# Local-attention layers: VectorE's chain of inverse norms issued behind the maximum and subtraction of the scores

## The reference

```python
def attn_layer(x, Wqkv, qs, ksc, Wo):
    q, k, v = jnp.split(x @ Wqkv, 3, -1)          # 16 heads of 64 each
    q = l2norm(q) * qs                            # t / max(norm(t), 1e-12), per head
    k = l2norm(k) * ksc
    q = q * cos * scale + rotate_half(q) * sin * scale
    k = k * cos * inv + rotate_half(k) * sin * inv
    out = local_attention(q, k, v)                # window 32, keys of this and the last window
    return out.transpose(0, 2, 1, 3).reshape(b, n, INNER) @ Wo

for i in range(DEPTH):                            # 6 layers
    x = attn_layer(shift_tokens(x), Wqkv[i], q_scale[i], k_scale[i], Wo[i]) + x
    x = ffn_layer(shift_tokens(x), ln_g[i], ln_b[i], W1[i], b1[i], W2[i], b2[i]) + x
```

## Time and profile before

| what | value |
|---|---|
| median of 3 runs | 4396.46 us (4378.6 to 4422.52) |
| the profiled execution | 4409.03 us |
| its span, first to last instruction | 4407.3 us |
| part B in it | about 1024 to 4330 us |
| mean granted TensorE clock | 0.906 of full speed |
| TensorE busy with matmuls | 3998.6 us, 91% |
| VectorE busy | 3520.4 us, 80% |
| GpSimd busy | 2552.0 us, 58% |
| ScalarE busy | 2544.9 us, 58% |

### The profile page before, as it was taken

How to read it: one execution, slowest core, us unless ns; L and a number is a source line. 1 busy time by engine, 2 the same in 40 slices (tenths; PEclk the granted TensorE clock), 3 DMA queues, 4 the chain that set the end, 5 groups by cost and what they waited for, 6 DMA issues and landing times. The chain is left out here.

```text
span 4407.3 us, 153325 instructions
## 1 busy us (share of the span) xinstructions
PE 3998.6 (91%) x66018; PEld 2914.3 (66%) x66018; DVE 3520.4 (80%) x5436; ACT 2544.9 (58%) x4654; POOL 2552.0 (58%) x1429
## 2 busy tenths in 40 slices
PE   7899999986998999999999999999999999999996
PEld 4555555545776777777776777777776777777774
DVE  5655555536888889999988898999988889998993
ACT  4544555534555666656656566666665566666563
POOL 2333333326666676667666666667766666666662
PEclk7866666658999999999999999999999999999997
DMA  1000000001211122221211122122121111212112
GB/s 46 4 3 2 2 2 2 3 26 41 54 49 48 48 54 55 53 56 48 62 54 47 49 54 54 52 56 56 48 54 52 51 54 49 56 50 53 50 48 61
DMA packets 122834, 188.19 MB, mean 43 GB/s; under 512 B 24910, under 2 KB 44134, under 8 KB 121964
## 3 DMA queue, kind: packets, MB, share of 16 engines
q1 hardware_dynamic: 122220, 179.07, 15.0%
HBM read 23.78 MB, written 4.19 MB: 6 GB/s over the span
## 5 line engine op out<-in xcount | busy, mean ns | idle before, releaser
L1251 POOL TENSOR_TENSOR rc<-rc,rnorm 128x1024 f32<-128x1024 f32 x384 | 734.5, 1933 | 358.5 <-DVE rnorm L205 358.5
L1245 POOL TENSOR_TENSOR rc<-rc,rs 128x1024 f32<-128x1024 f32 x384 | 905.2, 2369 | 34.5 <-DVE rs L1313 30.8
L1273 POOL TENSOR_TENSOR prob_b<-prob_b,rinv 128x1024 f32<-128x1024 f32 x192 | 365.9, 1906 | 653.0 <-DVE rinv L1386 653.0
L562 POOL TENSOR_TENSOR prob<-prob,rden 128x512 f32<-128x512 f32 (+3 forms) x128 | 297.6, 2325 | 661.3 <-DVE rden L674 661.3
L1307 DVE TENSOR_TENSOR rc<-proj,rope_b 128x1024 f32<-128x1024 f32 x384 | 469.2, 1222 | 114.9 <-PE proj L853 63.8
L941 PE MATMUL ring<-pT,vmoved 64*64 64x32 f32 x18432 | 436.0, 221 | 115.1 <-issue 113.8
L1093 ACT ACTIVATE oT_b<-ring 128x512 f32<-128x512 f32 x384 | 209.6, 596 | 564.6 <-PE ring L941 564.6
L941 PEld LDWEIGHTS ring<-pT,vmoved 64*64 64x64 f32 x18432 | 401.0, 135 | 179.5 <-issue 162.3
L890 PEld LDWEIGHTS ring<-ident,rc 128*128 128x128 f32 x3072 | 362.3, 143 | 235.5 <-POOL rc L1251 77.2
L890 PE MATMUL ring<-ident,rc 128*128 128x128 f32 x3072 | 455.9, 278 | 62.2 <-POOL rc L1251 59.4
L1321 DVE TENSOR_REDUCE sums<-squares 128x16 f32<-128x1024 f32 x384 | 460.2, 1198 | 44.5 <-ACT squares L1105 42.3
(11 more groups left out here) (163 smaller groups left out, 8837.0 us busy)
## 6 DMA issues: line engine op xcount, KB each, us to landing
vmoved<-vown SPq DMA_DIRECT2D x576, 128.0 KB, 2.4
vmoved<-vown SPq DMA_DIRECT2D x192, 192.0 KB, 2.5
vmoved<-vown SPq DMA_DIRECT2D x576, 64.0 KB, 2.1
wqkv_raw<-in_L_ffn_Wqkv SPq DMA_DIRECT2D x40, 192.0 KB, 2.7
wo<-in_L_ffn_Wo SPq DMA_DIRECT2D x6, 512.0 KB, 4.2
x_attended<-xtok SPq DMA_DIRECT2D x8, 256.0 KB, 2.0
xtok_c<-x_attended SPq DMA_DIRECT2D x8, 256.0 KB, 4.4
out<-xtok_c SPq DMA_DIRECT2D x8, 256.0 KB, 2.5
```

The source lines that it names most:

```text
L1245: nc.gpsimd.tensor_tensor(rc[:, k % 2, c, :], rc[:, k % 2, c, :], rs[:, c, :], ALU.add).then_inc(add_done, 1)
L1251: nc.gpsimd.tensor_tensor(dst, dst, rnorm[:, k % 2, c * HEADS:(c + 1) * HEADS].rearrange("p (h o) -> p h o", o=1).broadcast_to([P, HEADS, ...
L1273: nc.gpsimd.tensor_tensor(pr, pr, rinv[:, :, :].rearrange("p q (s o) -> p q s o", o=1).broadcast_to([P, PAIRS, 2, KEYS]), ALU.mult).then_i ...
```

## The change

In VectorE's list of every step, the call of `norms_of(g + 1, ...)` is moved from in front of the maximum and subtraction of tile g to behind them. Nothing is added, removed or resized, and the lists of the other engines stay as they are.

```diff
                 if tile(g + 1):
                     square_sums(1, g + 1)
-                if tile(g + 1) or seq_at(g, 6) is not None:
-                    norms_of(g + 1, seq_at(g, 6))
                 if tile(g):
                     dve.wait_ge(scr_full, g + 1)
                     nc.vector.tensor_reduce(rmax[:, :, :], scr[:, :, :, :], AX.X, ALU.max).then_inc(max_done, 1)
@@
                         prob[g % 2][:, :, :, :].rearrange("p q s k -> p s q k"), scr[:, :, :, :],
                         rmax[:, :, :].rearrange("p s (q o) -> p s q o", o=1).broadcast_to([P, 2, PAIRS, KEYS]),
                         ALU.subtract).then_inc(sub_done, 1)
+                if tile(g + 1) or seq_at(g, 6) is not None:
+                    norms_of(g + 1, seq_at(g, 6))
```

## The result

The changed kernel takes 4629.03 us (median of 4 runs, 4593.07 to 4641.46), the kernel before beside it 4409.49 us (4 runs). The ratio is 1.0494, 95% interval 1.0403 to 1.0585: slower, as forecast (4646 us; 1.057 of the median then shown). In a second job it was 4614.6 us, ratio 1.063 (1.0531 to 1.0729). Medians are of all runs, but a ratio takes only those within 1.5% of the fastest run of their kernel, which in the second job, by one run of 4310.12 us, are 5 of the 17 of the kernel before: there the medians themselves (4614.6 and 4380.57 us) have a ratio of 1.053. The profiled execution has a span of 4615.0 us at a mean clock of 0.902.

A forecast was written before the change was run, and what follows sets the result against it. Bound: TensorE back to back, caught at times by the chain norms, `scale_heads`, T1. Chain 205 plus clock 45 is 250 us on the profiled 4409, 4659; less 12.6 for the median, 4646 us, range 4546 to 4760.

The forecast's parts named there:

- The clamp: VectorE's clamp in its new place takes 0.18 us instead of 1.84, bounds 0.18 and 1.84.
- The chain behind the scores: Tiles 1 and 3: next masks 8.91 us after the scores end; steps grow by 2.38 and 1.55 us.
- The reserve of one tenth for covered waits: Pauses in `weigh` cover some of the new wait, so nine tenths of 225 us: 205 us.
- Tile 2: `spread` (L978), in front of the output projection, waits for the later copy: +0.76 us per sequence.
- one of the prediction's own signs of being wrong: In any step, scores ending earlier in their step than in the kernel before would make the prediction wrong.
- the sentence that what is freed comes back nowhere: TensorE, ScalarE and VectorE's rotations regain nothing elsewhere from what the change frees; no time credited.
- The clock: Behind TensorE's 96 new waits at T0 and T1, three in ten cost 1.6 us each: 45 us, from 0 to 154.
- tile 0's: Tile 0's step: the chain ends at 2918.76, masks were at 2918.80 anyway, so 0 added.
- B: Rival: VectorE bounds tiles 2 and 0, so its saving of 1.66 us each shortens them; 4237 us, chance 0.04.
- C: Rival: the clamp's 1.84 us is its own and moves with it into the chain; 4938 us, chance 0.05.
- D: Rival: most of TensorE's 147.6 us of pauses in `weigh` vanish; 4453 us or less, chance 0.05.

The follow-up runs named there:

- the norms in the middle: Against the kernel before: order maximum, norms, subtraction in all tiles; 4454.19 us, ratio 1.0183.
- the wait alone: Against the kernel before: its order kept, only a wait for the scores put in front of the norms; 4410.07 us against 4402.94, ratio 1.005.
- filled, second run: Changed kernel plus unused products in front of T0 and T1 in TensorE's waits of tiles 1 and 3, run again; 4525.43 us, ratio 1.0447 to the kernel before.
- the first experiment: Against the kernel before: norms behind maximum and subtraction only in tiles 1 and 3; 4612.53 us, ratio 1.051.
- low part later: Against the kernel before: GpSimd's second low part of the input (L1227) moved behind the scaling of the next step; 4359.18 us against 4377.84, ratio 1.0003.
- both edits: Against the kernel before: clamp left out and GpSimd's second low part moved behind the next scaling; 4355.02 us against 4380.57, ratio 1.0019.

## Why the prediction was right

The direction, the mechanism and the total came out; the terms of the sum did not all have their size. The total is closer than the forecast was: 250 us more were forecast and 219.5 measured (4629.03 - 4409.49). 4646 lies 17 us from 4629 because the median it was added to, 4396.46 us, was 13 us below the one measured beside the changed kernel. That is luck.

**The clamp.** Taken at 0.18 us, measured 0.171. That its 1.84 us were a stall behind GpSimd's add was argued from the ends of both; the runs without the clamp and with the add moved show it. One reading was off: what ends at 2861.39 in tile 1 is not an add of the halves but GpSimd's L1287 (from 2860.12), beside which the first guess took its 1.20 us. The time given to the clamp doesn't change by it.

**The chain behind the scores.** 8.91 us were predicted from the end of the scores to the next masks. In the step of tile 1 above, the last scores start at 2966.16 and take 0.86 us, as the next fence shows, and the masks come at 2975.82: 8.80 us. Tile 1 was to grow by 2.38 us and grew by 2.26 in the median, tile 3 by 1.55 and grew by 1.45. The reserve of one tenth for covered waits was about right too: 114 and 74 us before it, 102.6 and 71.5 measured. The experiment with the norms in the middle shows the slope, the one with the wait alone that it is the work behind the scores and not the wait.

**Tile 2** is the term that was mis-sized: +0.76 us through `spread`. In the changed kernel TensorE (first and last row) and VectorE read:

```profile
2966.16 0.86 PE L910 MATMUL scr<-kT,qT 64*32 64x64 f32 x64
...
2982.65 0.86 PE L910 MATMUL scr<-kT,qT 64*32 64x64 f32 x64
...
2983.55 1.22 DVE L1399 TENSOR_REDUCE rmax<-scr 128x16 f32<-128x1024 f32 x1 [0.74 <-PE scr L910]
...
2988.04 0.43 DVE L1343 COPY hid<-rnorm 128x512 f32<-128x512 f32 x1
...
2988.53 0.66 PE L978 MATMUL proj<-ident,hid 128*128 128x128 f32 x4 [0.26 <-DVE hid L1343]
```

The wait is there, but 0.26 us long, and it came in 26 of the 48 tiles 2, 12.1 us in all. The scores end 7.69 us into the step (2983.51 - 2975.82), in the kernel before 8.12. That the scores end earlier in their step was one of the prediction's own signs of being wrong; it came true in tile 2. In the kernel before, TensorE's weight loads wait twice in this step for ScalarE to empty a bank:

```profile
2868.22 0.42 PEld L890 LDWEIGHTS ring<-ident,rc 128*128 128x128 f32 x4 [0.31 <-ACT qT L1093]
...
2871.09 0.19 PEld L851 LDWEIGHTS ring<-wqkv_hi,xa_hi 128*128 128x128 f32 x1 [0.56 <-ACT qT L1093]
```

In the same step of the changed kernel neither wait is there: while TensorE waits in tile 1, VectorE and ScalarE get ahead. So the sentence that what is freed comes back nowhere was wrong. The medians of the steps that no low clock touches separate the two effects (us):

| kernel | tile 1 | tile 2 | tile 3 | tile 0 |
|---|---|---|---|---|
| before | 16.00 | 17.41 | 16.98 | 16.79 |
| norms behind only in tiles 1 and 3 | 18.27 | 17.07 | 18.43 | 16.66 |
| norms behind only in tiles 0 and 2 | 15.71 | 17.97 | 16.96 | 16.97 |
| changed | 18.27 | 17.55 | 18.43 | 16.62 |
| filled, second run | 18.27 | 17.56 | 18.43 | 16.61 |

A longer tile 1 alone gives tile 2 back 0.34 us, the late copy alone costs it 0.56, and both together 0.14.

**The clock** was taken somewhat too small: 45 us. Between the two kernels that ran side by side, the time at the low clock fell by 190 us (259 to 69) and part B by 84. That makes 0.44 us per us at the low clock; between the first traces of the two it was 65 us of part B for 140 at the low clock, 0.46. The changed kernel has 118 us more at it than the kernel before (114 to 232), in the second job 145 more (259), so that by this estimate the clock cost 52 and 64 us. There are 57 stretches at the low clock in its part B, 64 in the second job, against 27 before: 30 to 37 more for 96 pairs of waits, where three in ten were forecast, at about 1.7 us each, where up to 1.6 was. The rows behind the forecast were one fall and one stay; a third wait in the trace of the kernel before, 2.46 us long and ended at 1592.10, had a clock of 0.54 over the 3.4 us from 1591.50, a second fall. A wait in two pieces brings the clock down as well: this is one of the places, TensorE at the end of the step of tile 3 and the start of the next.

```profile
3009.42 0.66 PE L890 MATMUL ring<-ident,rc 128*128 128x128 f32 x4 [0.56 <-POOL rc L1251]
3011.28 1.12 PE L890 MATMUL ring<-ident,rc 128*128 128x128 f32 x4 [1.21 <-POOL rc L1251]
3012.19 1.06 PE L898 MATMUL scr<-masks 128*128 128x512 bf16 x2
```

```profile
3012.19:3015.59 3.40, 3.40 (x13) 0.64 0.01 2
```

The clock also explains tile 0 in the first experiment, 17.69 us instead of 17.20: without the steps at the low clock it is 16.66 us, in the kernel before 16.79.

**The sum.** Chain 205 us predicted (nine tenths of 225 are 203); measured 217.5 less the clock's 52, that is about 165, or, from the table above, 3.69 us per sequence instead of 4.69, that is 177. The part that is missing is tile 2's and a little of tile 0's. Clock 45 predicted, 52 to 64 measured. The two errors stand against each other, and part of the closeness of 4646 to 4629 is owed to that as well.

**The rivals.** B (VectorE bounds tiles 2 and 0) was refuted by the order changed only there. C (the clamp's time is its own) by its 171 ns in the new place and by the trace of the run without it. D (the pauses in `weigh` vanish) by the row of waits: 146.1 us, before 147.6. The rule of the Trainium skill, "Perfetto Trace Analysis", section "Identifying the Most-Contended Engine", would have led to B: in part B VectorE's occupancy fell from 2955 of 3306 us to 2605 of 3519, and the kernel became slower.

## What to carry to other kernels

An engine that is 89% busy needn't be the bound. Before moving an instruction on it, look for whom each result is waited for: here the norms had a consumer within 0.4 us of its limit and the subtraction had more than that to spare, so the order that keeps VectorE least busy was the worse one. An instruction put behind one that waits for another engine inherits that wait and all the work in between; count from the event waited for. If a change makes TensorE wait, count the clock behind the waits too; products without use in the wait gave back 1.9% here.

## What had not been expected of the hardware

- Products of no use make the changed kernel faster: 576 added matmuls, 89 us less, through 190 us less at the low clock. It stays slower than the kernel before.
- Two waits of 0.6 and 1.2 us with four transposes between them are enough for the low clock to follow, as above. The same pair in the step of tile 1 shown first was followed by full clock.
- An instruction on 32 numbers per row is held until GpSimd's add of 2.4 us beside it ends: on average 1.84 us for the clamp, 1.75 for the integer first guess in its place, against 0.17 and 0.18 alone. Whichever comes first takes the stall.
- Gains of 32, 33 and 39 us in part B (no clamp, low part later, both) came with medians 26, 19 and 26 us lower, which the ratios don't tell from nothing. Part A varies by more: the first masks of part B come at 965.9 us in one trace and at 1041.6 in another, with the same work in front of them. The windows of the first 965 us of two traces, the second filled run and the run with both edits, show TensorE's clock (the third value from the end) as the difference:

```profile
0.00:965.00 965.00, 818.37 (x5334) 474.49 (x5334) 542.12 (x1357) 491.88 (x1446) 318.45 (x158) 0.74 0.04 11
```

```profile
0.00:965.00 965.00, 863.37 (x5103) 494.09 (x5103) 525.20 (x1299) 477.51 (x1405) 292.67 (x131) 0.66 0.02 7
```

Why the clock in part A differs from execution to execution was not tried.
